# Another order of the first tile, and the last tile in three pieces from two queues

## The chip, the cores and the metric

The kernel runs on one core of one Trainium2 chip. The metric is the device time of one execution in microseconds (us). Lower is better.

## The reference

`x` has the shape (64, 64, 1024): batch, head, length. Each head has a state-space filter of 64 complex states, and each batch element a valid length. The filtered rows go through a feed-forward part with 64 experts of rank 16, of which each row takes the best 16. The result is added to `x`.

```python
u_m = u * mask[:, None, :]                       # mask: position < length
dt = exp(log_dt); A = -exp(log_A_real) + 1j * A_imag
K = 2 * real(einsum('hn,hnl->hl', C * (exp(A * dt) - 1) / A, exp(A * dt * arange(L))))
y = causal_convolution(u_m, K) + u_m * D         # by FFT in the reference
y = y * mask
scores = y @ Wr.T                                # 64 scores for each row of 1024
gates = softmax(top_k(scores, 16)) scattered to 64 columns, the others zero
h = einsum('nd,krd->nkr', y, A)                  # 1024 -> 64 x 16
out = x + 2 * einsum('nkr,kdr->nd', h * gates, B)
```

## The kernel before

**Tiles.** A tile holds two heads (`HT = 2`) of all 64 batch elements, which makes 128 rows; there are 32 tiles (`TILES`). A row of 1024 is cut into 8 chunks of 128 (`NC`).

**The convolution.** For tile t, ACT writes arguments (`theta`), DVE takes them to one turn (`arguments`), ACT makes sines and decays, DVE multiplies them to `powers` (`make_powers`) and to `out_raw` (`out_factors`). TensorE turns the powers (`turn_in`), sums `out_raw` to the filter's first 128 values, the kernel row (`whole_row`, later `kernel_row`), and feeds the states (`whole_feed`, `feed`). ACT copies the row to `k_sb` (`copy_k`), DVE adds the skip weight D to one element per head (`add_skip`), and SP starts two DMAs (`load_near`) that read `k_sb` shifted by one element for each of 128 partitions, and so write the Toeplitz matrix `t_lo`. Then TensorE convolves the chunk with itself (`near`, for tile 0 `whole_near_0`) and adds what the states carry over from earlier chunks (`from_states`, `whole_from_states_0`). DVE steps the states from chunk to chunk (`first_states`, `states`, each step some 1.3 us long in two heads). `mask_y` (for tile 0 `mask_first`) writes the masked rows `y_m`.

**The feed-forward part.** TensorE multiplies `y_m` by the A weights and the router in three column ranges (`H_PARTS`, n = 0, 1, 2). DVE finds the gates (`gate`, `gates_of`) and multiplies each range by them (`gate_part`, into `hg`). TensorE turns `hg` (`turn_hg`), ACT and DVE split it into `g_hi` and `g_lo` (`low_gated`), and TensorE multiplies by the B weights into `out_ps`, in halves of 512 columns (`down_high`, `down_low`). `add_rows` scales, adds x, and SP stores the rows.

**Precision.** From tile 2 on, every product is three products of rounded parts (high by high, high by low, low by high). Tiles 0 and 1 (`EXACT = 2`) use whole float32 operands for A and the convolution, and split ones for B. So all weights have to be split in the first two tiles: ACT rounds a piece to its high part (`split_weights`), DVE subtracts it from the original for the low part (`low_weights`). There are 17 pieces: the router, eight of A, eight of B. Four pieces of B (`EARLY`) have their low parts made by TensorE instead (`whole_b`: the identity times the piece, plus minus the identity times its high part), and ACT copies them out of PSUM.

**Order.** Everything is written out by hand. SP issues the loads in the order of `EARLY`, five of the first pieces, `load_near(0)`, the rest of A, `MIDST` (the other four of B), the x rows. Each engine's queue is in order, and semaphores link them. TensorE begins with `whole_b(0)`, then alternates pieces of B with the first tile's row and feed, does `whole_near_0` and `whole_from_states_0(0)`, and goes on with `first_step` (tile 0's products, the convolution of tile 1, the preparation of tile 2), `step(1, whole=True)`, then a loop of `step(t)`. The last tile runs the same `step` without convolution.

## Time and profile before

| | |
|---|---|
| median of three runs | 953.88 us (953.48 to 954.99) |
| profiled execution, whole time | 952.23 us |
| its span, first to last instruction | 950.4 us |
| TensorE busy | 924.9 us, 97% of the span |
| VectorE (DVE) busy | 701.0 us, 74% |
| ScalarE (ACT) busy | 393.0 us, 41% |
| mean granted TensorE clock | 0.996 of full |

The span is what the profiler sees of the program; 1.8 us of the whole time lie outside it. The busy time of an engine is the union of its instructions, and the page names for idle time what ended it. "PE" is TensorE's matmuls, "PEld" its weight loads, which overlap them. "ACTq" and "SPq" are the engines' instruction queues, where they issue DMAs. A float32 matmul is two instructions in the trace.

### The profile page before, as it was taken

The page shows a single profiled execution, that of the slowest core. Times are in us where ns is not written, and L with a number is a line of the kernel's source. Part 1 is how long each engine was busy: PE and PEld are TensorE (multiplying, and loading weights), DVE is VectorE, ACT ScalarE, POOL GpSimd, SP SyncE. Part 2 cuts the span into 40 slices and gives each one's busy share as a digit, 9 for nine tenths or more (in the row PEclk, how much of TensorE's full clock was granted, in tenths as well). Part 3 has the DMA queues.
Part 4 walks back from the last instruction along what each step waited for, and adds up shares of the span by engine and source line. Part 5 has one row for each costly group of instructions (what it writes and reads, how often), then busy time and mean ns, then how long its engine had stood idle before and what let it go on. Part 6 is the DMA issues. An engine that isn't in the chain of part 4 may idle for free.

```text
span 950.4 us, 15672 instructions
## 1 busy us (share of the span) xinstructions
PE 924.9 (97%) x4772; PEld 819.2 (86%) x4772; DVE 701.0 (74%) x2443; ACT 393.0 (41%) x685; POOL 2.0 (0%) x12
## 2 busy tenths in 40 slices
PE   4899999999999999999999999999999999999998
PEld 2567888899998899998899998889999889999887
DVE  7678977787777788777778777778877778877642
ACT  4655344334344434344434434443534443443210
POOL 0000000000000000000000000000000000000000
PEclk9999999999999999999999999999999999999999
DMA  6713232222332222332222333222233222233211
GB/s 220 227 28 73 53 81 50 56 64 56 72 72 50 48 68 50 72 72 51 49 66 52 68 72 70 51 48 69 50 72 72 50 48 67 50 72 72 34 40 45
DMA packets 27983, 63.60 MB, mean 67 GB/s; under 512 B 5184, under 2 KB 13504, under 8 KB 27968
## 3 DMA queue, kind: packets, MB, share of 16 engines
q1 hardware_dynamic: 27696, 63.29, 30.0%
q8 instruction: 7, 0.11, 0.0%
q10 hardware_dynamic: 272, 0.13, 0.0%
q14 instruction: 8, 0.07, 0.0%
HBM read 42.43 MB, written 16.78 MB: 62 GB/s over the span
## 4 chain that ended last, share of the span: by engine, by line
PE 93%; DVE 4%; DMA 1%; ACT 1%; issue 0%; ACTq 0%; SPq 0%; DVEq 0%
PE out_ps L926 23%; PE h_ps L926 18%; PE out_ps L930 12%; PE h_ps L930 9%; PE turn_ps L926 7%; PE turn_ps L930 4%; PE turn_ps L948 3%; PE h_ps L935 2%; PE conv_ps L881 1%; PE conv_ps L880 1%; PE conv_ps L879 1%; PE conv_ps L863 1%; PE conv_ps L890 1%; PE conv_ps L891 1%; PE conv_ps L864 1%; PE conv_ps L862 1%
## 5 line engine op out<-in xcount | busy, mean ns | idle before, releaser
L926 PE MATMUL out_ps<-b_hi,g_hi 128*128 128x512 f32 x512 | 203.3, 397 | 0.2 <-ACT g_hi L401 0.2
L926 PE MATMUL out_ps<-b_lo,g_hi 128*128 128x512 f32 x512 | 201.1, 393 | 0.0
L743 DVE SCALAR_TENSOR_TENSOR x_in<-out_ps,gate_scale,x_in 128x512 f32<-128x512 f32 x64 | 48.0, 750 | 160.5 <-PE out_ps L930 160.4
L926 PE MATMUL h_ps<-a_hi,y_hi 128*128 128x384 f32 x480 | 163.3, 340 | 0.0
L926 PE MATMUL h_ps<-a_lo,y_hi 128*128 128x384 f32 x480 | 161.6, 337 | 0.0
L930 PE MATMUL out_ps<-b_hi,g_lo 128*128 128x512 f32 x512 | 127.3, 391 | 0.0
L930 PEld LDWEIGHTS out_ps<-b_hi,g_lo 128*128 128x128 f32 x512 | 96.1, 188 | 21.2
L926 PEld LDWEIGHTS out_ps<-b_hi,g_hi 128*128 128x128 f32 x512 | 96.3, 188 | 19.4 <-ACT g_hi L401 0.5
L926 PEld LDWEIGHTS out_ps<-b_lo,g_hi 128*128 128x128 f32 x512 | 96.3, 188 | 19.2
L542 DVE SCALAR_TENSOR_TENSOR z<-swapped,step_other,part 128x64 f32<-128x64 f32 x384 | 92.4, 282 | 11.4
L535 DVE SCALAR_TENSOR_TENSOR part<-z,step_own,conv_ps 128x64 f32<-128x64 f32 x384 | 90.4, 277 | 8.6
L930 PE MATMUL h_ps<-a_hi,y_lo 128*128 128x384 f32 x480 | 94.4, 338 | 0.0
L926 PEld LDWEIGHTS h_ps<-a_lo,y_hi 128*128 128x128 f32 x480 | 90.1, 188 | 0.0
L926 PEld LDWEIGHTS h_ps<-a_hi,y_hi 128*128 128x128 f32 x480 | 90.0, 187 | 0.0
L930 PEld LDWEIGHTS h_ps<-a_hi,y_lo 128*128 128x128 f32 x480 | 85.3, 188 | 0.0
L401 ACT ACTIVATE g_hi<-turn_ps 128x512 fp32r<-128x512 f32 x64 | 38.3, 601 | 113.2 <-PE turn_ps L948 113.2
L335 ACT ACTIVATE k_sb<-h_ps 1x256 f32<-1x256 f32 x31 | 11.7, 376 | 148.7 <-PE h_ps L850 144.4
L926 PE MATMUL turn_ps<-a_hi,y_hi 128*128 128x320 f32 x240 | 71.0, 309 | 1.7 <-DVE a_lo L571 1.7
L926 PE MATMUL turn_ps<-a_lo,y_hi 128*128 128x320 f32 x240 | 70.8, 309 | 0.0
L343 ACT ACTIVATE z_hi<-z 128x896 fp32r<-128x896 f32 x30 | 28.6, 954 | 87.0 <-DVE z L542 87.0
L391 ACT ACTIVATE exp_all<-score_sb,neg_max 128x64 f32<-128x64 f32 x32 | 11.2, 348 | 116.8 <-DVE neg_max L700 116.8
L537 DVE STREAM_SHUFFLE swapped<-z 128x128 f32<-128x128 f32 x192 | 57.0, 297 | 0.0
(198 smaller groups left out, 1504.9 us busy)
## 6 DMA issues: line engine op xcount, KB each, us to landing
xt_in<-in_xt SPq DMA_DIRECT2D x32, 512.0 KB, 3.3
x_in<-in_x SPq DMA_DIRECT2D x64, 256.0 KB, 3.7
out<-x_in SPq DMA_DIRECT2D x62, 256.0 KB, 4.3
b_in<-in_b_t SPq DMA_DIRECT2D x8, 512.0 KB, 8.5
a_in<-in_a_t SPq DMA_DIRECT2D x8, 512.0 KB, 7.6
t_lo<-k_sb SPq DMA_DIRECT2D x64, 64.0 KB, 5.5
out<-x_in SPq DMA_DIRECT2D x4, 128.0 KB, 2.3
a_in<-in_wr_t SPq DMA_DIRECT2D x1, 256.0 KB, 9.0
```

The costliest lines, as they stand in the source:

```text
L335: act.activation(k_sb[:, :, PAD:PAD + P], source[0:1, :, :], ACT.Copy).then_inc(s_kcopy, 1)
L343: act.activation(z_hi[:, :, :, :], z[:, :, :, :], ACT.Copy).then_inc(s_zhi, 1)
L391: act.activation(exp_all[:, :], score_sb[:, :], ACT.Exp, bias=neg_max[:, :]).then_inc(s_exp, 1)
L401: act.activation(g_hi[:, 4 * bank:4 * bank + 4, :].rearrange("p c n -> p (c n)"), turn_ps[:, bank, :], ACT.Copy).then_inc(s_ghi, 1)
L535: dve.scalar_tensor_tensor(out=part[:, i, :], in0=z[:, c - 1, i, :], scalar=step_own[:, bass.ds(n + i, 1)], in1=conv_ps[i][:, c * B:(c + 1 ...
L537: dve.stream_shuffle(swapped[:, :, :], z[:, c - 1, :, :], SWAP).then_inc(s_swap, 1)
L542: dve.scalar_tensor_tensor(out=z[:, c, i, :], in0=swapped[:, i, :], scalar=step_other[:, bass.ds(n + i, 1)], in1=part[:, i, :], op0=ALU.mu ...
L743: dve.scalar_tensor_tensor(out=x_in[:, columns], in0=out_ps[:, half, :], scalar=gate_scale[:, :], in1=x_in[:, columns], op0=ALU.mult, op1= ...
L926: pe.matmul(o, hi[:, c, :], moving[:, c, columns], start=first and c == order[0] and moving is w_hi, stop=False)
L930: last = pe.matmul(o, lo[:, c, :], w_hi[:, c, columns], start=False, stop=c == order[-1])
L935: return pe.matmul(o, y_m[:, c, :], a_in[:, c, c0:c0 + width], start=c == 0, stop=c == NC - 1)
L948: last = pe.transpose(turn_ps[:, c // 4, (c % 4) * P:(c % 4 + 1) * P], hg[:, c * P:(c + 1) * P], ident[:, :])
```

## The change

Five things change together.

1. The first arguments are made by ACT (`theta(0)`), no longer by two DVE instructions; `phases` goes. DVE does the weights alpha and beta before anything of the far steps, which move behind `out_factors(0)`. TensorE does `turn_in(0)`, `whole_row(0)`, `whole_feed(0)` before any piece of B. ACT copies the row before it makes `far_sin`. The load of the lengths and the first split of a weight move behind `theta(0)` in ACT's queue.
2. `k_sb` is on all 128 partitions. `load_near` reads head 0 from partition 0 and head 1 from partition 64.
3. The first tile's convolution is done in halves: `whole_near_0(0)`, `whole_from_states_0(0)`, `whole_near_0(1)`.
4. `EARLY` is one piece of B instead of four. The other seven are `MIDST`, and DVE makes their low parts. The loads have a new order: that piece, seven of router and A, `load_near(0)`, three of B, the last two of A, four of B. ACT splits nine pieces (router and A) in tile 0's step: two before `g_hi`, seven behind `theta(3)`. DVE's and TensorE's orders in `first_step` change too: `turn_hg` in two parts between products.
5. The last tile has a `last_step` of its own: the first `turn_hg` lies inside the third range of the A product, and the output is made in three pieces (`ENDS`: 512, 256 and 256 columns, the last in `h_ps`). Each piece is stored by two DMAs, head 0 from SP, head 1 from ACT.

```diff
-        k_sb = sb("k_sb", [1, HT, KROW])
+        k_sb = sb("k_sb", [P, HT, KROW])
...
+        ENDS = [(out_ps[:, 0, :], slice(0, HALF)), (out_ps[:, 1, 0:HALF // 2], slice(HALF, HALF + HALF // 2)),
+                (h_ps[:, 0, 0:HALF // 2], slice(HALF + HALF // 2, D))]
...
-        EARLY = [FIRST_B + c for c in (4, 5, 6, 7)]
-        MIDST = [FIRST_B + c for c in (3, 2, 1, 0)]
+        EARLY = [FIRST_B + c for c in (4,)]
+        MIDST = [FIRST_B + c for c in (5, 6, 7, 3, 2, 1, 0)]
         LATE = list(range(FIRST_B))
-        HIGH = EARLY + LATE[:3] + MIDST + LATE[3:]
+        HIGH = EARLY + MIDST + LATE
...
-                    row = k_sb[:, i, :]
+                    row = k_sb[i * B:i * B + 1, i, :]
...
-            for i in range(5):
+            for i in range(7):
                 load_weights(i)
             load_near(0, first=True)
-            for i in range(5, FIRST_B):
-                load_weights(i)
-            for i in MIDST:
+            for i in MIDST[:3] + LATE[7:] + MIDST[3:]:
                 load_weights(i)
...
-                    for half in range(2):
-                        sp.wait_ge(s_o, 2 * t + half + 1)
-                        columns = slice(half * HALF, (half + 1) * HALF)
-                        for i in range(HT):
-                            sp.dma_start(rows(out, t, i)[:, columns], x_in[i * B:(i + 1) * B, columns]).then_inc(s_out, 16)
+                    for n, (_, columns) in enumerate(ENDS):
+                        sp.wait_ge(s_o, 2 * t + n + 1)
+                        sp.dma_start(rows(out, t, 0)[:, columns], x_in[0:B, columns]).then_inc(s_out, 16)
...
-                act.activation(k_sb[:, :, PAD:PAD + P], source[0:1, :, :], ACT.Copy).then_inc(s_kcopy, 1)
+                act.activation(k_sb[:, :, PAD:PAD + P], source, ACT.Copy).then_inc(s_kcopy, 1)
...
-            act.dma_start(len_i[:, :], length.partition_broadcast(P)).then_inc(s_len, 16)
-            split_weights(EARLY[0])
             act.wait_ge(s_rates, 1)
...
+            theta(0)
+            act.dma_start(len_i[:, :], length.partition_broadcast(P)).then_inc(s_len, 16)
+            split_weights(EARLY[0])
             sines(0)
+            whole_in(0, in_ps)
+            copy_k(0)
             act.wait_ge(s_far, 1)
             act.activation(far_sin[:, :, :], far_turn[:, :, :], ACT.Sin, scale=TWO_PI).then_inc(s_farwave, 1)
             theta(1)
-            whole_in(0, in_ps)
-            split_weights(EARLY[1])
             low_weights(0)
-            split_weights(EARLY[2])
-            copy_k(0)
-            low_weights(1)
-            split_weights(EARLY[3])
-            low_weights(2)
-            low_weights(3)
-            for i in LATE[:3] + MIDST[:2]:
+            for i in MIDST[:3]:
                 split_weights(i)
             sines(1)
+            decays(1)
             theta(2)
-            decays(1)
-            for i in MIDST[2:] + LATE[3:6]:
+            for i in MIDST[3:]:
                 split_weights(i)
...
                     copy_k(1, k_ps_1)
+                    for i in LATE[:2]:
+                        split_weights(i)
...
                 if first:
-                    for i in LATE[6:]:
-                        split_weights(i)
+                    decays(2)
                     sines(2)
                     theta(3)
-                    decays(2)
+                    for i in LATE[2:]:
+                        split_weights(i)
...
+            for n, (_, columns) in enumerate(ENDS):
+                act.wait_ge(s_o, 2 * (TILES - 1) + n + 1)
+                act.dma_start(rows(out, TILES - 1, 1)[:, columns], x_in[B:HT * B, columns]).then_inc(s_out, 16)
...
-            for i in range(HT):
-                dve.scalar_tensor_tensor(out=args[:, i], in0=grid[:, :].unsqueeze(1).to_broadcast([P, 2, W]), scalar=turns[:, i:i + 1],
-                                         in1=phases[:, :, :], op0=ALU.mult, op1=ALU.add).then_inc(s_theta, 2)
...
             first_states(0)
-            states(0, range(1, 2))
-            add_skip(0)
-            states(0, range(2, 5))
+            states(0, range(1, 3))
...
+            states(0, range(3, 4))
             mask_first(0)
-            states(0, range(5, FED))
+            states(0, range(4, FED))
             arguments(1)
-            for i in MIDST[:2]:
+            mask_first(1)
+            for i in MIDST[:3]:
                 low_weights(i)
-            mask_first(1)
             make_powers(1)
             out_factors(1)
-            for i in MIDST[2:]:
+            for i in MIDST[3:5]:
                 low_weights(i)
...
                 sum_gates()
+                arguments(2)
+                low_weights(MIDST[5])
                 first_states(1)
+                states(1, range(1, 2))
                 add_skip(1)
-                states(1, range(1, 3))
+                low_weights(MIDST[6])
                 gate_part(0, 2)
-                states(1, range(3, 5))
                 low_gated(0, 0)
+                states(1, range(2, 4))
                 low_gated(0, 1)
-                states(1, range(5, FED))
-                arguments(2)
+                states(1, range(4, FED))
...
+                        if n == 2 and c == NC - 2:
+                            pe.wait_ge(s_hg, 2)
+                            turn_hg((7, 6, 5, 4)).then_inc(s_turn, 1)
...
-                pe.wait_ge(s_hg, 3)
-                turn_hg((7, 6, 5, 4)).then_inc(s_turn, 1)
-                turn_hg((3, 2, 1, 0)).then_inc(s_turn, 1)
                 pe.wait_ge(s_ghi, 1)
                 pe.wait_ge(s_kcopy, 2)
+                pe.wait_ge(s_wlo, 3)
+                down_high(0, (4, 5, 6, 7), first=True)
+                pe.wait_ge(s_hg, 3)
+                turn_hg((3, 2, 1, 0)).then_inc(s_turn, 1)
+                down_high(1, (4, 5, 6, 7), first=True)
+                pe.wait_ge(s_ghi, 2)
                 pe.wait_ge(s_wlo, len(MIDST))
-                for half in range(2):
-                    down_high(half, (4, 5, 6, 7), first=True)
-                pe.wait_ge(s_ghi, 2)
                 down_high(0, (0, 1, 2, 3))
...
+            def last_step(t):
+                pe.wait_ge(s_yhi, HT * (t - EXACT) + HT)
+                pe.wait_ge(s_glo, 2 * t)
+                pe.wait_ge(s_ylo, HT * (t - EXACT) + HT)
+                for n, (o, c0, width, _) in enumerate(H_PARTS):
+                    columns = slice(c0, c0 + width)
+                    product_high(o, y_hi, a_hi, a_lo, columns, range(NC), first=True)
+                    if n == 2:
+                        pe.wait_ge(s_hg, 3 * t + 2)
+                        turn_hg((7, 6, 5, 4)).then_inc(s_turn, 1)
+                    product_low(o, y_lo, a_hi, columns, range(NC)).then_inc(s_up, 1)
+                pe.wait_ge(s_ghi, 2 * t + 1)
+                pe.wait_ge(s_o, 2 * t)
+                for n, (o, columns) in enumerate(ENDS):
+                    if n == 1:
+                        pe.wait_ge(s_hg, 3 * t + 3)
+                        turn_hg((3, 2, 1, 0)).then_inc(s_turn, 1)
+                    product_high(o, g_hi, b_hi, b_lo, columns, (4, 5, 6, 7), first=True)
+                pe.wait_ge(s_ghi, 2 * t + 2)
+                for n, (o, columns) in enumerate(ENDS):
+                    product_high(o, g_hi, b_hi, b_lo, columns, (0, 1, 2, 3))
+                    if n == 0:
+                        pe.wait_ge(s_glo, 2 * t + 2)
+                    product_low(o, g_lo, b_hi, columns, (4, 5, 6, 7, 0, 1, 2, 3)).then_inc(s_down, 1)
+
             pe.wait_ge(s_ident, 2)
             pe.wait_ge(s_minus, 3)
+            turn_in(0)
+            whole_row(0, k_ps)
+            whole_feed(0)
             whole_b(0)
-            turn_in(0)
-            whole_b(1)
-            whole_feed(0)
-            whole_row(0, k_ps)
-            whole_b(2)
-            whole_b(3)
-            whole_near_0()
+            pe.wait_ge(s_t, 16 * HT)
+            whole_near_0(0)
             whole_from_states_0(0)
+            whole_near_0(1).then_inc(s_near, 1)
             first_step()
...
-            step(TILES - 1, conv=False, prep=False)
+            last_step(TILES - 1)
```

## Rows read from the trace of the kernel before

**Rows 1.** The page: busy time, share of the span, instructions of TensorE.

```profile
PE 924.9 (97%) x4772; PEld 819.2 (86%) x4772; DVE 701.0 (74%) x2443; ACT 393.0 (41%) x685; POOL 2.0 (0%) x12
```

**Rows 2.** Waits of TensorE in the whole span: us in total, times, longest.

```profile
PE turn_ps L835 <- ACT b_hi L289: 10.9, 1, 10.9
PE out_ps L899 <- DMA t_lo<-k_sb: 3.2, 1, 3.2
...
PE turn_ps L926 <- DVE a_lo L571: 1.7, 1, 1.7
```

**Rows 3.** Windows: stretch, length, busy time by engine, PEclk, DMA share, GB/s.

```profile
36.40:73.50 37.10, 35.23 (x134) 24.07 (x135) 28.52 (x96) 24.49 (x38) 0.00 (x0) 1.00 0.36 95
...
162.50:190.70 28.20, 28.20 (x152) 25.64 (x151) 21.32 (x75) 12.01 (x22) 0.00 (x0) 1.00 0.28 60
```

**Rows 4.** Timeline of TensorE, the first 37 us: start, us, instruction, idle before.

```profile
17.03 1.66 PE L835 MATMUL out_ps<-b_in,ident 128*128 128x512 f32 x2 [1.79 <-ACT b_hi L289]
...
20.98 1.67 PE L872 MATMUL conv_ps<-xt_in,in_whole 128*128 128x448 f32 x4
22.48 0.59 PE L854 MATMUL h_ps<-out_raw,real 128*128 128x256 f32 x2
22.91 1.02 PE L835 MATMUL turn_ps<-b_in,ident 128*128 128x512 f32 x2
...
31.20 3.63 PE L899 MATMUL out_ps<-xt_in,t_lo 128*128 128x256 f32 x8 [3.25 <-DMA t_lo<-k_sb]
...
36.44 0.78 PE L935 MATMUL turn_ps<-a_in,y_m 128*128 128x320 f32 x2 [0.96 <-issue]
```

**Rows 5.** Timeline of ACT: one instruction of `theta`, and the row's copy.

```profile
14.12 0.48 ACT L303 ACTIVATE args<-grid,phase_own,turns 128x130 f32<-128x130 f32 x1
...
23.11 0.38 ACT L335 ACTIVATE k_sb<-h_ps 1x256 f32<-1x256 f32 x1 [4.23 <-PE h_ps L854]
```

**Rows 6.** Timeline of DVE up to 42 us.

```profile
10.67 0.89 DVE L618 SCALAR_TENSOR_TENSOR args<-grid,turns,phases 128x260 f32<-128x260 f32 x2
...
18.48 0.61 DVE L492 SCALAR_TENSOR_TENSOR out_raw<-powers,alpha,out_raw 128x130 f32<-128x130 f32 x2
...
24.14 0.14 DVE L506 TENSOR_TENSOR k_sb<-k_sb,skip 1x2 f32<-1x2 f32 x1
...
39.83 2.35 DVE L571 TENSOR_TENSOR b_lo<-b_in,b_hi 128x1024 fp32r<-128x1024 f32 x2
```

**Rows 7.** DMA between 24 and 32 us, in 40 slices of 0.2 us.

```profile
GB/s 0 0 0 0 0 0 0 18 28 33 26 26 26 23 23 23 26 23 31 28 23 26 28 23 26 23 28 23 23 28 82 149 274 448 369 430 410 471 348 430
```

**Rows 8.** Windows: the stretch in which `whole_near_0` runs.

```profile
31.20:34.50 3.30, 3.30 (x8) 2.67 (x9) 0.00 (x0) 0.28 (x1) 0.00 (x0) 0.50 1.03 420
```

**Rows 9.** Timelines in `first_step` and at the start of `step(1)`.

```profile
46.09 2.94 ACT L289 ACTIVATE a_hi<-a_in 128x1024 fp32r<-128x1024 f32 x3
...
55.44 1.09 PE L948 MATMUL turn_ps<-ident,hg 128*128 128x128 f32 x8 [1.11 <-DVE hg L723]
...
70.86 1.22 DVE L515 TENSOR_TENSOR xt_lo<-xt_in,xt_hi 128x1024 fp32r<-128x1024 f32 x1
...
73.50 4.47 PE L935 MATMUL turn_ps<-a_in,y_m 128*128 128x320 f32 x16
```

**Rows 10.** Two matmuls of 256 columns behind each other.

```profile
99.19 0.28 PE L849 MATMUL h_ps<-o_hi,real 128*128 128x256 f32 x1
99.30 0.28 PE L850 MATMUL h_ps<-o_lo,real 128*128 128x256 f32 x1
```

**Rows 11.** The last tile: timelines of TensorE, DVE and SP.

```profile
934.61 0.66 PE L948 MATMUL turn_ps<-ident,hg 128*128 128x128 f32 x4 [0.21 <-DVE hg L723]
...
946.40 0.75 DVE L743 SCALAR_TENSOR_TENSOR x_in<-out_ps,gate_scale,x_in 128x512 f32<-128x512 f32 x1 [2.80 <-PE out_ps L930]
947.18 1.11 SPq L252 DMA_DIRECT2D out<-x_in  x2
```

**Rows 12.** Groups by line and form from 890 us on: a DVE instruction on 256 columns.

```profile
L723 DVE TENSOR_TENSOR hg<-turn_ps,gates 128x256 f32<-128x256 f32 x2 | 0.8, 425 | 0.1
```

More of the change, by code:

```diff
@@ L295, in low_weights @@
                 for half in range(2):
-                    act.activation(lo[:, half * HALF:(half + 1) * HALF], REST_PS[n][:, half, :], ACT.Copy).then_inc(s_blo, 1)
+                    act.activation(lo[:, half * HALF:(half + 1) * HALF], turn_ps[:, half, :], ACT.Copy).then_inc(s_blo, 1)
             def theta(t):
-                act.wait_ge(s_sine, t)
+                if not (isinstance(t, int) and t == 0):
+                    act.wait_ge(s_sine, t)
                 for i in range(HT):
@@ L668, in _ @@
             out_factors(0)
+            link(dve.tensor_scalar(far[:, 1, :], turns[:, :], float(P), None, ALU.mult))
+            dve.tensor_scalar(whole[:, 1, :], far[:, 1, :], ROUND, ROUND, ALU.add, ALU.subtract)
+            link(dve.tensor_scalar(far[:, 0, :], far[:, 1, :], 0.25, None, ALU.add))
+            link(dve.tensor_scalar(whole[:, 0, :], far[:, 0, :], ROUND, ROUND, ALU.add, ALU.subtract))
+            dve.tensor_tensor(out=far_turn[:, :, :], in0=far[:, :, :], in1=whole[:, :, :], op=ALU.subtract).then_inc(s_far, 1)
+            add_skip(0)
             dve.wait_ge(s_farwave, 2)
@@ L772, in first_step, with step @@
                 add_rows(0, 1)
-            def step(t, conv=True, prep=True, table=True, weights=()):
+            def step(t, conv=True, prep=True, table=True, weights=(), last=False):
                 if conv:
@@ L811, in step @@
                 scale_of(t)
+                if last:
+                    for n in range(len(ENDS)):
+                        add_rows(t, n, ENDS)
+                    return
                 add_rows(t, 0)
@@ L822, in _ @@
             step(TILES - 2, prep=False, table=False)
-            step(TILES - 1, conv=False, prep=False, table=False)
+            step(TILES - 1, conv=False, prep=False, table=False, last=True)
         @block.tensor
@@ L834, in whole_b @@
                     columns = slice(half * HALF, (half + 1) * HALF)
-                    pe.matmul(REST_PS[n][:, half, :], ident[:, :], arrived[:, columns], start=True, stop=False)
-                    last = pe.matmul(REST_PS[n][:, half, :], minus[:, :], hi[:, columns], start=False, stop=True)
+                    pe.matmul(turn_ps[:, half, :], ident[:, :], arrived[:, columns], start=True, stop=False)
+                    last = pe.matmul(turn_ps[:, half, :], minus[:, :], hi[:, columns], start=False, stop=True)
                 last.then_inc(s_rest_ps, 1)
@@ L891, in from_states, with whole_near_0 @@
                     pe.matmul(later, o_lo[:, i, 1:P + 1], z_hi[:, :, i, :], start=False, stop=True).then_inc(s_conv, 1)
-            def whole_near_0():
-                pe.wait_ge(s_t, 16 * HT)
-                pe.wait_ge(s_blo, 2 * len(EARLY))
-                for n in range(2):
-                    columns = slice(n * HALF // 2, (n + 1) * HALF // 2)
-                    for i in range(HT):
-                        last = pe.matmul(conv_0[n][:, i, :, :], t_lo[:, i, :].bitcast(F32), xt_in[:, i, columns],
-                                         start=i == 0, stop=False, skip_group_check=True)
-                last.then_inc(s_near, 1)
+            def whole_near_0(n):
+                columns = slice(n * HALF // 2, (n + 1) * HALF // 2)
+                for i in range(HT):
+                    last = pe.matmul(conv_0[n][:, i, :, :], t_lo[:, i, :].bitcast(F32), xt_in[:, i, columns],
+                                     start=i == 0, stop=False, skip_group_check=True)
+                return last
             def whole_from_states_0(n):
@@ L958, in first_step @@
                 pe.wait_ge(s_w[0], 16)
+                pe.wait_ge(s_blo, 2 * len(EARLY))
                 pe.wait_ge(s_ym0, HT)
```

53 lines of the change are left out of this document (19 added, 34 removed).

## The prediction

> **What bounds the kernel now.** I read the page first: TensorE is busy 97% of the span [rows 1]. Then I asked where its missing 25.5 us lie, by its waits over the whole span [rows 2] and by windows [rows 3]. In the loop there is nothing to win: of a stretch of 28.20 us TensorE is busy 28.20 [rows 3]. No row of waits belongs to the loop either. So the time is TensorE's work, plus what it stands still in the first 106 us, plus the tail behind its last matmul. The waits at the start are 10.9 us for the first piece of B, 3.2 us for `t_lo`, 1.7 us for `a_lo` [rows 2] and some smaller ones. Third I followed the timelines of the first 37 us. TensorE works early, but on pieces of B; the chain that counts is another: kernel row at 22.48 [rows 4], its copy at 23.11 [rows 5], the skip weight at 24.14 [rows 6], the load of `t_lo`, the convolution at 31.20, the products of tile 0 at 36.44 [rows 4]. From there to the loop TensorE is nearly full, so what is gained ahead of 36.44 counts, less what later waits take back.
>
> **Part 1, the row first.** The turns are ready at 10.55. The two instructions on `args`, 0.89 us [rows 6], leave DVE; five small ones on the far steps (0.7 together) move behind. ACT makes the arguments instead: behind the sine table, which it can load earlier since the first split of B (1.0 us) is no longer ahead, it does two sines, then four of `theta` at 0.4 us each [rows 5], so they are there at about 12.7. DVE has by then done the weights up to the fraction (13.3 or so), so it doesn't wait; it ends `out_raw` at about 17.8 instead of 19.1 [rows 6]. Ahead of TensorE's row there is now no piece of B and no feed. The row takes 0.59 us at the full clock [rows 4]; TensorE has only just begun, so I take 1.0. It ends at 18.9, where it ended at 23.07. Copy 0.38, skip 0.14 and the gaps between them [rows 5, 6] put the issue of the load at 19.6 instead of 24.3: 4.7 us earlier. The next work of TensorE, feed (1.67) and `whole_b(0)` (2.2: two halves, each little more than the 1.02 of its first two instructions [rows 4]), ends at 24 to 26 us, by the clock. The lengths' load moved behind `theta(0)` is 32 KB that took 5.9 us to land; DVE needs it at 25, so it costs nothing; without that cover it would be DVE that waits.
>
> **Part 2, two partitions.** The two transfers move 128 KB in 5.3 us, from 25.7 to about 31, at 18 to 33 GB/s, while the weights behind them go at 348 to 471 [rows 7]. The source is one partition, and both transfers go one after the other through the same rings. From two partitions they could overlap, but only as far as engines run ahead into the second: the rate rises from 28 to 448 over some 0.8 us at the end [rows 7], which is how far apart they finish. I take 0.5 us; the bounds are nothing and 2.1 (half of 5.3, less the 0.6 by which the second is issued later). So `t_lo` is there at 31.2 - 4.7 - 0.5 = 26.0. The Trainium skill (SBUF — State Buffer, Door 1: The DMA port swizzle) says that partitions 64 apart lie on different ports of 27.2 GB/s each. The row's rate agrees with one port; no row here shows two. By that rule, with both ports in use at once, the 128 KB would take 2.4 us, an estimate from its figure; what the rows make of such an overlap is rival (c). `k_sb` on 128 partitions costs ACT nothing that a row shows: the same copy with more partitions is what every other ACT row is.
>
> **Part 3, halves.** `whole_near_0` took 3.63 us at half the clock [rows 4, 8]; a matmul of 256 columns at the full clock takes 0.11 a pass [rows 10], and a whole one two passes, so 1.8 for all eight. TensorE now does half (0.9), the states (0.6), then the other half (0.9) while DVE masks the first. Before, it stood 0.96 us for that mask [rows 4]. With `t_lo` at 26.0 the first half and states end at 27.5, the second half and the mask (0.7) at 28.4: the products start at 28.4 instead of 36.4, 8.0 us earlier. DVE would be ready for the mask at about 26.9 (feed ended 22, three steps of the states, the mask's making), so more than 0.6 us cannot come from a faster `t_lo`. The clock: before, TensorE stood 3.25 us and ran the convolution at 0.50 [rows 4, 8], and it stood 1.79 before 17.03 [rows 4] and ran those pieces slowly too. Now it stands up to 2 us. I take the full clock and keep 1.5 us for the other case (0.9 for half the convolution, 0.6 for its states).
>
> **Part 4, the weights.** DVE gets three more pieces of B, at 2.35 us for two [rows 6] 3.5 us, and one more step of the states (1.3) falls behind the first mask. From that mask to the end of `xt_lo` at 72.1 [rows 9] DVE was busy some 28 us (28.52 in [rows 3], less its last 1.4, plus the mask); now 32.7. It had 8.5 us of idleness in that stretch, so the queue takes it, but DVE is now what times it. Piece by piece: masks and states to 33.8; three pieces of B to 37.3; powers and `out_raw` to 38.9; two pieces to 41.2. TensorE's range 0 is done at 38.8, so the gates start 2.4 us late (before, 1.3). That is hidden, since TensorE has ranges 1 and 2, feed and row until 46.6. Then the fixed order bites: arguments, a piece of B, first states, a step, the skip, another piece, and only then the third `gate_part`, at 49.9, while TensorE wants to turn at 48.5: it waits 1.4. The wait of 1.11 at 55.44 [rows 9] goes in exchange, and so does most of the turning behind it. The convolution of tile 1 waits 0.7 for the last steps of the states. ACT has seven splits of A (0.98 each by 2.94 for three [rows 9], 6.8) behind `theta(3)`; queued behind them are `o_hi`, `in_hi`, `xt_hi`, which come at 63.7 at the latest, so `xt_lo` ends at 64.9, and TensorE's feed, ready at 64.3, waits 0.6. `step(1)` starts at 66.1 instead of 73.50 [rows 9]: of the 8.0 us, 0.6 are given back, 7.4 stay. Loads: behind `t_lo` go 4.5 MB of weights, the x rows and `xt` of tile 1, at 0.4 MB per us [rows 7]; a half MB takes 1.3 us, so the last of A lands at 32.7 (needed at 37), the last of B at 37.8, `xt` at 39.7 (needed at 41.5). In `step(1)` the nine `a_lo` are the same, behind the same `turn_hg`, so that wait of 1.7 stays.
>
> **Part 5, the tail.** The first `turn_hg` moves into the product (0.44 in place of a wait of about as much), the second lies between pieces and waits for nothing, so the idle 0.21 and the ramp behind it [rows 11] go: 0.4 us. The 48 matmuls of 256 columns cost as much as 24 of 512, at 0.11 each [rows 10]; the bound on the other side is a pass of 320 columns, 0.14 (4.47 for 16 instructions of two passes [rows 9]), which would add 1.4 us. The last scaling is half as wide: 0.75 [rows 11] becomes 0.43 [rows 12]. One issue is left on each queue: 1.11 for two [rows 11] becomes 0.56. The landing of 2.1 us stays. Sum: 0.4 + 0.3 + 0.55 = 1.3 us less. The bounds are 1.8 less, were the landing half a microsecond shorter for half the bytes, and 0.1 more, with the narrow passes at 0.14.
>
> **The sum.** 7.4 + 1.3 = 8.7 us. The profiled execution of 952.2 us becomes 943.5. The three runs have a median 1.7 us above it, 953.88; so the forecast is 945.2 us. A measurement of this kernel tells 0.2%, 1.9 us, from no change.
>
> **The rivals.** (a) The forecast, 0.52: 945.2, by itself 943.8 to 946.8. (b) The clock is down when `t_lo` comes, 0.18: 1.5 us later masks, and DVE's queue passes it on whole: 946.7. For it: 1.79 us of idleness was enough once [rows 4]. Against: the new gap is shorter if `whole_b` runs slowly. (c) Both rows are read side by side, 0.12: `t_lo` at 31.2 - 4.7 - 2.1 = 24.4; DVE caps it at 0.6 us: 944.6, or 943.1 if my DVE times are late. (d) The queues behind take more: ACT's seven splits, or a load that misses its time by 1.3 us per half MB, hold feed or gates of tile 0 by 2 to 4 us more than I have, 0.10: 948.5. (e) The narrow matmuls run at 0.14, or the small stores land later, 0.05: 946.7 to 947.5. (f) Slower: the loop. If the wider `k_sb` made the row late in each tile, the 29 tiles would repeat it. It decides from 0.4 us a tile (11.6 us): 956. It needs the copy, the skip or the load to eat the slack of `t_lo`, and TensorE has no idle time in a tile that would show it near [rows 3]: 0.03.
>
> **Range and chances.** (a), (b), (c) and (e) lie within 943.0 to 947.5; the upper end goes to 948.8 to take in most of (d). Faster 0.94, same 0.03, slower 0.03.
>
> **What would show it.** Right: TensorE's order row, feed, one piece; the issue of `t_lo` at 19 to 20 us, the first half at 25 to 27, the products at 28 to 29, `step(1)` at 65 to 67.5; `hg` or `xt_lo` as the new short waits; 3.2 us from the last matmul to the end of the span, instead of 4.0. Wrong: a PEclk of 0.50 around 26 to 30 us, a wait for a load at the ranges of A, matmuls of 256 columns further apart than 0.12, a tile of the loop longer than 28.2.

## The result, and the profile after

The changed kernel takes 943.02 us (median of four runs, 942.97 to 943.06), against 953.68 us for the kernel before in the same job (953.11 to 954.99). The ratio is 0.9886, interval 0.9869 to 0.9903. In a second job it took 943.06 us (942.96 to 943.16), against 951.43 for the kernel before (median of 23 runs, 950.52 to 954.99), ratio 0.9906. The forecast was 945.2 with a range of 943.0 to 948.8. The kernel is faster, as forecast, and its time is 2.2 us below the forecast: at the very edge of the range, and below the 943.8 to 946.8 that the forecast had by itself. The gain is 10.7 us where 8.7 were forecast.

The profiled execution took 942.97 us with a span of 941.2, against 952.23 and 950.4: 9.26 us less. The waits of TensorE over its whole span come first, in the columns of [rows 2]:

```profile
PE h_ps L838 <- DVE powers L479: 16.2, 1, 16.2
PE turn_ps L918 <- DVE a_lo L571: 1.7, 1, 1.7
PE out_ps L891 <- DMA t_lo<-k_sb: 1.3, 1, 1.3
PE conv_ps L867 <- issue: 1.2, 1, 1.2
PE conv_ps L908 <- DVE part L535: 0.7, 1, 0.7
PE turn_ps L940 <- DVE hg L714: 0.6, 1, 0.6
PE conv_ps L857 <- issue: 0.6, 1, 0.6
```

TensorE waits longer at the very start (16.2 us, where 10.9 stood in [rows 2]), since it no longer does pieces of B there. The wait for `t_lo` has fallen from 3.2 to 1.3, and the wait for `a_lo` stayed. Behind it stand short new waits: `hg`, `part`, and two that the profile puts down to nothing ("issue"). Of these the 1.2 us are for the load of `xt` (`e8_xt_early` below takes them away), and the 0.6 us end at 64.10, just behind DVE's `xt_lo` (from 62.77, 1.23 us long). The timeline of TensorE, for [rows 4]:

```profile
17.47 1.22 PE L849 MATMUL h_ps<-out_raw,real 128*128 128x256 f32 x2 [0.57 <-DVE out_raw L492]
18.49 2.75 PE L867 MATMUL conv_ps<-xt_in,in_whole 128*128 128x448 f32 x4
21.08 1.02 PE L830 MATMUL turn_ps<-b_in,ident 128*128 128x512 f32 x2
...
24.72 1.13 PE L891 MATMUL out_ps<-xt_in,t_lo 128*128 128x256 f32 x4 [1.30 <-DMA t_lo<-k_sb]
25.69 0.81 PE L901 MATMUL out_ps<-z,out_raw 128*128 128x192 f32 x4
26.34 1.03 PE L891 MATMUL out_ps<-xt_in,t_lo 128*128 128x256 f32 x4
27.55 0.78 PE L927 MATMUL turn_ps<-a_in,y_m 128*128 128x320 f32 x2 [0.19 <-DVE y_m L559]
...
42.17 1.74 PE L867 MATMUL conv_ps<-xt_in,in_whole 128*128 128x448 f32 x4 [1.25 <-issue]
...
65.39 4.47 PE L927 MATMUL turn_ps<-a_in,y_m 128*128 128x320 f32 x16
```

The order is row, feed, one piece of B, half the convolution, states, other half. The products start at 27.55 where they started at 36.44, and `step(1)` at 65.39 where it started at 73.50 [rows 9]. Of 8.89 us gained ahead of the products, 0.78 are given back up to `step(1)`. The loop is the same, and so is the clock, by these windows of the kernel after (columns of [rows 3]):

```profile
36.00:65.39 29.39, 26.87 (x106) 18.35 (x105) 25.08 (x81) 20.80 (x33) 0.00 (x0) 1.00 0.29 66
154.40:182.60 28.20, 28.20 (x152) 25.64 (x151) 21.35 (x75) 12.02 (x22) 0.00 (x0) 1.00 0.26 60
```

DVE is busy 25.08 of the 29.39 us ahead of `step(1)`, 85%, where it was 28.52 of 37.10 [rows 3], 77%. The end, for [rows 10] and [rows 11]; the first two rows are matmuls of the last piece:

```profile
936.67 0.28 PE L918 MATMUL h_ps<-b_hi,g_hi 128*128 128x256 f32 x1
...
936.79 0.28 PE L918 MATMUL h_ps<-b_lo,g_hi 128*128 128x256 f32 x1
...
938.07 0.48 DVE L734 SCALAR_TENSOR_TENSOR x_in<-h_ps,gate_scale,x_in 128x256 f32<-128x256 f32 x1 [1.43 <-PE h_ps L922]
```

DVE starts the last scaling at 938.07, 3.1 us before the span ends at 941.2; before, it started at 946.40 [rows 11], 4.0 before the end at 950.4.

### The profile page after: what moved, and what is told of

It is laid out like the page before. It is cut to its first block, busy times and chain, and to the rows that moved or that the text cites. A ratio compares the mean times of both kernels' runs of the same rounds, so it can differ in the third digit from the quotient of the medians.

```text
span 941.2 us, 15678 instructions
## 1 busy us (share of the span) xinstructions
PE 914.9 (97%) x4778; PEld 815.3 (87%) x4778; DVE 704.8 (75%) x2442; ACT 389.1 (41%) x681; POOL 2.0 (0%) x12
## 4 chain that ended last, share of the span: by engine, by line
PE 92%; DVE 6%; DMA 1%; issue 0%; ACT 0%; ACTq 0%; SPq 0%; DVEq 0%
PE out_ps L918 23%; PE h_ps L918 18%; PE out_ps L922 12%; PE h_ps L922 9%; PE turn_ps L918 8%; PE turn_ps L922 4%; PE turn_ps L940 3%; PE conv_ps L876 1%; PE conv_ps L875 1%; PE conv_ps L874 1%; PE conv_ps L857 1%; PE conv_ps L858 1%; PE conv_ps L885 1%; PE conv_ps L859 1%; PE conv_ps L886 1%; PE conv_ps L884 1%
## 5 line engine op out<-in xcount | busy, mean ns | idle before, releaser
L922 PE MATMUL out_ps<-b_hi,g_lo 128*128 128x512 f32 (+1 forms) x512 | 126.4, 389 | 0.0
L335 ACT ACTIVATE k_sb<-h_ps 128x256 f32<-128x256 f32 x31 | 12.0, 387 | 144.9 <-PE h_ps L845 143.5
```

What stands on the lines that cost most here:

```text
L335: act.activation(k_sb[:, :, PAD:PAD + P], source, ACT.Copy).then_inc(s_kcopy, 1)
L922: last = pe.matmul(o, lo[:, c, :], w_hi[:, c, columns], start=False, stop=c == order[-1])
```

## The experiments

Each stands beside runs of the kernel before in the same job; the jobs ran on three chips. The kernel after itself ran in two jobs only, 943.02 us in the first and 943.06 in the second (`e1_tail_alone` to `e4_after_again`). Where a run of a later job is compared with it, the difference leans on how close these two are, and on the profile. "Products" is the start of tile 0's products on TensorE, "step(1)" that of `step(1)`, both in the profile. Dummy matmuls, where a kernel has them, write to PSUM that nothing reads; the rest of the computation is as it was.

### The parts by themselves: tail, partition, halves, pieces of B

Part 1, the row first, has no run of its own. Its worth is read from the timelines alone.

**`e1_tail_alone`**: the kernel before with part 5 of the change only (`ENDS`, `last_step`, the stores from ACT).

```diff
-                add_rows(t, 0)
...
+                if last:
+                    for n in range(len(ENDS)):
+                        add_rows(t, n, ENDS)
+                    return
```

> The kernel before with part 5 alone (the last tile in three pieces, two queues). Theory: the tail is additive, since its trace in the changed kernel ends 3.2 us behind the last matmul where it ended 4.0 before: 1.1 us less than the kernel before in the profiled span, nothing else moves. Rival (the narrow matmuls cost more than they bring, and the gain of the tail belongs to the start): no difference, within 0.3 us. If the changed kernel's further gain over my sum lies in the tail, this shows over 2 us.

Measured: 949.88 us (949.36 to 953.75, 12 runs) against 951.43, ratio 0.999 (0.9979 to 1.0001). The medians differ by 1.5 us, but both scatter by over 4. The profile is sharper: from the start of `step(1)`, 72.06, to the end of the span, 947.8, there are 875.7 us, where there were 876.9 before (950.4 less 73.50). The tail is worth 1.2 us, 1.1 in the kernel after (941.2 less 65.39 is 875.8). The same profile holds a surprise: nothing at the start had changed, and yet `step(1)` came 1.4 us earlier than in [rows 9]. Here are windows over the second piece of B, which stands ahead of feed and row in TensorE's queue, first of the kernel before, then of this one:

```profile
17.50:20.80 3.30, 3.30 (x6) 0.50 0.44 170
```

```profile
17.50:20.80 3.30, 3.30 (x10) 1.00 0.43 166
```

One execution has the clock at 0.50 (1.2 GHz) there and does six instructions, the other has 1.00 (2.4 GHz) and does ten. The kernel row follows: 22.48 in [rows 4], 21.15 here.

**`e2_one_partition`**: the kernel after, both heads' rows read from partition 0.

```diff
-                    row = k_sb[i * B:i * B + 1, i, :]
+                    row = k_sb[0:1, i, :]
```

> The changed kernel, but both rows of k_sb are read from partition 0. Theory: two source partitions let the two transfers overlap, 3.8 us instead of 5.3; undone, t_lo lands 1.5 us later at 26.2, the first mask waits for it, and the time is 1.2 us longer (1.5 less the 0.3 that DVE was not ready anyway), more if TensorE's clock falls in the longer wait (up to 1.5 more). Rival (the shorter load comes from an idle DMA system, not from the partitions): the load still takes 3.8 us and the time does not change.

Measured: 944.43 to 944.49 in four runs, 945.72 and 945.75 in two, against 943.06 for the kernel after. Timeline of TensorE in one of the longer kind, and the window of its second half of the convolution:

```profile
26.23 1.13 PE L891 MATMUL out_ps<-xt_in,t_lo 128*128 128x256 f32 x4 [2.93 <-DMA t_lo<-k_sb]
27.20 1.42 PE L901 MATMUL out_ps<-z,out_raw 128*128 128x192 f32 x4
28.41 1.91 PE L891 MATMUL out_ps<-xt_in,t_lo 128*128 128x256 f32 x4
```

```profile
28.10:29.90 1.80, 1.80 (x6) 0.50 1.04 426
```

`t_lo` comes 1.5 us later than in the kernel after (26.23 against 24.72), and behind a wait of 2.9 us the clock fell to 0.50 at about 27 us; `step(1)` is at 68.16. So the second partition is worth 1.4 us by itself, and it takes away a further risk: rival (b), at 1.3 us, happened in two runs of six here and in none of the nine runs of the kernel after.

**`e7_no_halves`**: the kernel after, whole convolution first, then the states.

```diff
-            whole_from_states_0(0)
             whole_near_0(1).then_inc(s_near, 1)
+            whole_from_states_0(0)
```

> The changed kernel with both halves of whole_near_0 ahead of the states' part. Theory: TensorE stands for the mask again and the mask comes 0.9 us later; DVE's queue passes 0.9 us on to the end: 943.9. Rival (DVE's later slack takes it): under 0.3 us.

Measured: 943.82 us (943.77 to 943.93), 0.8 more than the kernel after. Its timeline:

```profile
24.70 1.99 PE L891 MATMUL out_ps<-xt_in,t_lo 128*128 128x256 f32 x8 [1.09 <-DMA t_lo<-k_sb]
26.53 0.81 PE L901 MATMUL out_ps<-z,out_raw 128*128 128x192 f32 x4
28.39 0.78 PE L927 MATMUL turn_ps<-a_in,y_m 128*128 128x320 f32 x2 [1.05 <-DVE y_m L559]
```

The wait for the mask is 1.05 us, where it is 0.19 in halves, and the products come 0.84 later. The halves are worth just that, and it reaches the end whole: `step(1)` is at 66.21, 0.82 later.

**`e12_four_by_tensor`**: the main thing of part 4 undone in the kernel after: four pieces of B by TensorE, the loads in their old order. The place of ACT's splits of A and the divided `turn_hg` stay as in the change. The cut shows the pieces alone.

```diff
-        EARLY = [FIRST_B + c for c in (4,)]
+        EARLY = [FIRST_B + c for c in (4, 5, 6, 7)]
...
             whole_b(0)
+            whole_b(1)
+            whole_b(2)
+            whole_b(3)
```

> The changed kernel with part 4 undone: four pieces of B by TensorE ahead of the convolution, the loads in their old order, no piece of B for DVE in tile 0's step. Theory: the convolution starts at 30 instead of 24.7 us, but DVE has 3.5 us less, so TensorE times the stretch: step(1) at 69 to 70 instead of 65.4, 4 us longer (947). Rival (part 4 brings nothing, since DVE gets what TensorE loses): within 1.5 us of 943.0.

Measured: 947.04 us (946.66 to 947.73), 4.0 more than the kernel after. The first half of the convolution stands at 31.11 behind the pieces, 6.4 later than in the kernel after, the products at 33.84, `step(1)` at 70.13. Of 6.3 us of TensorE's work in front of the products 4.7 reach `step(1)`, in a profiled execution of 947.73, the longest of the six; the other 1.6 come back before `step(1)`.

**`e11_two_by_tensor`**: the same with two pieces (`EARLY` of 4 and 5).

> The changed kernel with two pieces of B by TensorE instead of one. Theory (DVE times the stretch, and TensorE stands 1.3 us before t_lo anyway): DVE has 1.15 us less, TensorE's second piece ends 0.7 us after t_lo; together 0.3 to 0.6 us shorter. Rival (TensorE's time ahead of the convolution is the scarcer): 0.5 us or more longer.

Measured: 943.34 us (942.87 to 943.89, 5 runs), no difference that this spread can tell from 943.06. The second piece lies in the wait for `t_lo`, which is gone; the half starts at 25.40 instead of 24.72, the products at 28.13 instead of 27.55, and `step(1)` at 65.29 instead of 65.39. DVE has one piece less, and what the products lose comes back in its queue. One piece or two is even here.

### What holds tile 0's stage

**`e8_xt_early`**: in the kernel after, `xt` of tile 1 loaded ahead of the last two pieces of B and of the x rows.

```diff
-            for i in MIDST[:3] + LATE[7:] + MIDST[3:]:
+            for i in MIDST[:3] + LATE[7:] + MIDST[3:5]:
                 load_weights(i)
-            fetch_rows(0)
             sp.wait_ge(s_near, 1)
             load_x(1)
+            for i in MIDST[5:]:
+                load_weights(i)
+            fetch_rows(0)
```

> The changed kernel, with the load of xt of tile 1 ahead of the last two pieces of B and the x rows. In the profile that load took 13.3 us and TensorE stood 1.25 us for it at 40.9. Theory (DVE's third gate_part at 49.0 is what TensorE would wait for instead): the wait at 40.9 goes, one of 1.0 to 1.3 appears ahead of the second turn_hg, and the time stays within 0.2 us. Rival (the load binds): 0.9 to 1.25 us shorter.

Measured: 943.0 us (942.94 to 943.36), no change. Its waits of TensorE:

```profile
PE turn_ps L942 <- DVE hg L716: 1.6, 2, 1.0
PE conv_ps L910 <- DVE part L537: 0.7, 1, 0.7
PE conv_ps L859 <- issue: 0.6, 1, 0.6
```

The wait of 1.2 us for `xt` is gone, and 1.0 us more are waited for `hg`; `step(1)` starts at 65.39 as before. The load was late, but the stage is timed by DVE. **`e4_after_again`**, the kernel after unchanged in the second job, says the same by chance:

> The changed kernel unchanged, for the size of the difference on this chip and the spread. Theory A: 943.0 within 0.2 us in every run, and the runs of the kernel before between 952 and 955.5, with the lower granted clock in the longer ones. Rival B: the runs of before differ without a difference of clock.

There the load came earlier (its wait was 0.36 us), `hg` was waited for 0.73, and `step(1)` was at 65.42. Its five runs lie within 0.2 us, as theory A had it; those of the kernel before go down to 950.52, below the 952 of the theory, and the longest have the lowest clock (0.994 from 953.05 us on).

**`e3_before_filled`**: the kernel before with three dummy matmuls of 512 columns in its wait for `t_lo`.

```diff
             whole_b(3)
+            for _ in range(3):
+                pe.matmul(h_ps[:, 0, :], ident[:, :], xt_in[:, 0, :], start=True, stop=True)
             whole_near_0()
```

> The kernel before, with three matmuls of 512 whole columns (2.8 us, result unused) in the time in which TensorE waits for t_lo, so that its clock does not fall. Theory A (the clock at half in whole_near_0 cost the kernel before 1.8 us there, and where its windows fall differs from run to run, which is the spread of 1.9 us in its runs): whole_near_0 takes 1.8 instead of 3.6 us, the time is 1.5 to 2 us shorter in the profile, up to 2.5 in the median, and the runs lie within 0.3 us of each other. Rival B (the spread is of DMA or of the start, not of the clock): whole_near_0 is shorter but the runs scatter as before by over 1 us.

Measured: 951.43 us (950.32 to 953.84, 12 runs), the same as the kernel before. The wait was filled and the clock stayed up, and it bought nothing; nor did the runs draw together, as rival B had it. They lie 3.5 us apart, and the three shortest (950.32 to 950.68) and the two longest (953.54 and 953.84) all have a mean granted clock of 1.00. Timeline, and waits of TensorE, in the profiled execution (950.86 us):

```profile
30.13 1.99 PE L899 MATMUL out_ps<-xt_in,t_lo 128*128 128x256 f32 x8 [0.66 <-DMA t_lo<-k_sb]
```

```profile
PE turn_ps L948 <- DVE hg L723: 1.9, 3, 1.1
...
PE conv_ps L872 <- ACT in_whole L327: 1.0, 1, 1.0
```

The convolution takes 1.99 us instead of 3.63 [rows 4], the products start at 33.74, but `step(1)` at 72.13, the same as with the slow convolution in `e1_tail_alone` (products 34.97, `step(1)` 72.06). A new wait of 1.0 for ACT's `in_whole` takes it. ACT in turn had stood for a piece of B, here until 36.50, and in the kernel before:

```profile
37.55 1.06 ACT L289 ACTIVATE b_hi<-b_in 128x1024 fp32r<-128x1024 f32 x1 [6.07 <-DMA b_in<-in_b_t]
```

That piece is queued on SP behind `load_near(0)`, which waits for the row. So in the kernel before, too, an earlier product is worth nothing by itself: ACT's queue, and the load it stands for, have to be earlier as well. In the change the pieces of B leave TensorE's and ACT's queues at the same place.

### Why the kernel before scatters

Its 23 runs in the second job go from 950.52 to 954.99, the kernel after's five within 0.2 us. `e3_before_filled` above and the next two kernels ask whether TensorE's clock in the first 35 us is the cause; then the same is tried on the kernel after.

**`e5_before_warmed`**: the kernel before with 18 small dummy matmuls at its very start.

> The kernel before, with 18 small matmuls of the identity by itself (result unused) from 3.3 us on, ahead of its first piece of B, so that the clock has risen when the work begins. Theory C (the spread of the kernel before, 950.5 to 955.0, comes from where in its first 20 us the clock rises: the filled wait for t_lo did not remove it, 950.3 to 953.8): the pieces of B run at full clock from the first on, the row ends at 20.5 to 21.5 us, all runs lie within 0.5 us of each other between 949.5 and 951. Rival D (the spread comes from the loads or from DVE and ACT at the start): it stays over 1.5 us wide.

Measured: 953.58 us (952.96 to 955.14, 12 runs) against 952.42, 1.1 longer (ratio 1.0014, interval 1.0001 to 1.0027): the opposite of a gain, and still 2.2 us wide. In the waits between 13.5 and 17.3 us the clock fell again (PEclk 0.83 there, 0.50 from 17.3 to 21.7), the row came at 23.77 and `step(1)` at 74.84. Three executions now stand in a line (`e1_tail_alone`, the kernel before, this one): row 21.15, 22.48, 23.77 and `step(1)` 72.06, 73.50, 74.84. The loads link the two: `t_lo` is issued at 22.98, 24.31 and 25.61, and the piece of B queued behind it, for which ACT stands, is there at 36.20, 37.55 and 38.84, each time 13.2 us later.

**`e9_before_kept_busy`**: dummies also in the two waits ahead of the row and, not in the cut, the three of `e3_before_filled` in that for `t_lo`. "(dummy)" stands for a matmul of the identity by itself.

```diff
             pe.wait_ge(s_minus, 3)
+            for _ in range(18): (dummy)
             whole_b(0)
+            for _ in range(5): (dummy)
             turn_in(0)
+            for _ in range(7): (dummy)
             whole_b(1)
```

> The kernel before with unused small matmuls wherever TensorE waits in the first 31 us: 18 at the start, 5 and 7 around turn_in(0), three wide ones before whole_near_0. The warm-up at the start alone made it longer (953.6), since the clock fell again in the waits at 13.5 to 17.3 and the row came at 23.8 instead of 22.5. Theory C (where the clock stands between 17 and 24 us sets the row's time, and the row's time sets the rest: row at 21.15, 22.48, 23.77 goes with step(1) at 72.06, 73.50, 74.84): the row is at 21.1 in every run, and all runs lie within 0.5 us of 950.3. Rival D: the spread stays over 1.5 us.

Measured: 951.79 us (951.40 to 952.12, 11 runs; a twelfth of 3309.8 is left out), while the kernel before went from 950.31 to 955.19 in the same job. Timeline:

```profile
19.32 1.66 PE L872 MATMUL conv_ps<-xt_in,in_whole 128*128 128x448 f32 x4
20.82 0.59 PE L854 MATMUL h_ps<-out_raw,real 128*128 128x256 f32 x2
...
33.14 0.78 PE L935 MATMUL turn_ps<-a_in,y_m 128*128 128x320 f32 x2 [0.97 <-issue]
```

With the clock up throughout (1.00 in each window to 34.5 us), the scatter is 0.7 us instead of 4.9, and instead of the 3.5 of `e3_before_filled`, which lacks only the dummies ahead of the row. Above 952.12 lie ten of the 17 runs of the kernel before in this job, two of the 12 of `e3_before_filled`, and none here: the long runs go with the waits in which TensorE stood idle, and with its slow pace behind them. That all of this is the granted clock isn't shown: in `e3_before_filled` runs 3.5 us apart have the same mean clock, and of the kernel before in the job of `e5_before_warmed` one run of 951.13 and one of 953.97 both have 0.998.

The level is not as expected: the row is the earliest of all, but `step(1)` is at 72.81, since ACT waits for a piece of B until 37.2 us and TensorE then for `in_whole`, 1.2. That piece comes 14.6 us behind the issue of `t_lo` at 22.64, not 13.2. A later load that binds in this way may also be what evens out the short end of the scatter; the runs don't tell these two apart. The fastest runs of the kernel before are 1.1 to 1.5 us below this kernel; why the load is late here isn't shown.

**`e6_after_warmed`** has 20 dummies ahead of `turn_in(0)` in the kernel after, and **`e10_after_kept_busy`** 22 there, 3 behind it, and 9 behind `whole_b(0)`.

> The changed kernel, with 20 such matmuls from 8.5 us to at most 16 us, ahead of turn_in(0). The profile has row and feed of tile 0 at half the clock (1.0 and 2.75 us instead of 0.5 and 1.5). Theory: DVE times this stretch; the states of tile 0 come 1.5 us earlier and t_lo 0.5 us, so the first mask comes about 0.5 us earlier, and 0.4 to 0.6 us go over to the end (942.5). Rival (DVE has slack there, t_lo or the loads bind): no change within 0.15.

> The changed kernel with 22 unused small matmuls from 8.5 us, 3 before the row, 9 before the wait for t_lo. The warmed one had two kinds of runs, 942.4 and 943.9, and in the profile a wait of 2.4 us for t_lo. Theory (the clock falls in that wait in some runs): all runs at 942.4 within 0.2 us. Rival (another cause of two kinds): both kinds stay.

Measured: `e6_after_warmed` 942.39 and 942.42 in two runs, 943.81 to 943.95 in three. The feed takes 1.67 us instead of 2.75 and the products start at 27.00, which is the gain of 0.6; but an earlier end of TensorE's work makes the wait for `t_lo` 2.4 us, and in three runs the mean clock reads 0.998. `e10_after_kept_busy`: 943.26 us (942.42 to 945.41, 6 runs), two of them at 0.998 and 945.1 or more. Its profile has the products at 27.19 and `step(1)` at 65.44. The products are 0.36 us earlier than in the kernel after and `step(1)` is no earlier: the wait for `xt`, ready at 42.30, has grown to 1.75 us. Filling the waits made the kernel after less steady, 3.0 us wide where it was 0.2; both kinds of runs stayed, as the rival had it, and what lets the clock fall in its two longer runs stays open.

### Two queues, and the three together

**`e14_two_queues`**: in the kernel after, head 1's first transfer of `t_lo` is issued by ACT behind `far_sin`, head 0's by SP as before. The access patterns are shortened to "...".

```diff
-                for i in range(HT):
+                for i in range(1 if first else HT):
...
+            act.wait_ge(s_kdone, 1)
+            act.dma_start(t_lo[:, 1, :]..., k_sb[B:B + 1, 1, :]...).then_inc(s_t, 16)
             theta(1)
```

> The changed kernel with the second row's load of t_lo in tile 0 issued by ACT instead of SP, so that the two transfers needn't go one after the other through the same rings. The two took 5.3 us from one partition and 3.8 from two. Theory (the source partition is the limit, 128 KB at 24.7 GB/s from one, and what is left of the 3.8 is that the rings work through the first before the second): both together in 2.7 to 3.3 us, t_lo 0.3 to 0.8 us earlier; DVE is ready for the mask 0.3 us ahead, so 0.3 us at most reach the end. Rival (3.8 us is a limit of small packets, not of order): the same 3.8 us.

Measured: 943.63 us (943.59 to 943.71), 0.6 longer than the kernel after. Both are issued at 19.40. The median time from issue to landing, in the kernel after, then here:

```profile
t_lo<-k_sb SPq DMA_DIRECT2D x2, 64.0 KB, 4.4
```

```profile
t_lo<-k_sb SPq DMA_DIRECT2D x1, 64.0 KB, 4.0
t_lo<-k_sb ACTq DMA_DIRECT2D x1, 64.0 KB, 6.0
```

SP's half lands at 23.4, ACT's at 25.4, and TensorE starts the convolution at 25.47, where it is 24.72 with both from SP; `step(1)` is at 66.14 for 65.39. Why the second queue is slower here isn't shown; that the weights' traffic shares with it from 22.6 us on is a suspicion.

**`e13_combined`**: two pieces by TensorE, `xt` early, 20 dummies ahead of `turn_in(0)`.

> The changed kernel with three edits of the experiments together: 20 unused small matmuls from 8.5 us, two pieces of B by TensorE, the load of xt of tile 1 ahead of the last two pieces of B. Theory: the small matmuls bring the feed 1.5 us forward (942.4 in the warmed kernel's faster runs), and the second piece fills the 2.4 us in which its clock fell in the other runs. All runs at 942.0 to 942.5. Rival: DVE's and ACT's queues take all of it, 942.9 or more, or two kinds of runs remain.

Measured: 942.31 us (941.82 to 942.68, 4 runs), ratio 0.989 to the kernel before (0.9873 to 0.9906): the lowest median of all, 0.7 below the kernel after in the other jobs. Three of its four runs lie just outside the 942.0 to 942.5 of the theory. The dummies bring `t_lo` forward, the second piece covers the wait (0.20 left, 2.4 in `e6_after_warmed`), and none of the four runs has the clock down:

```profile
24.27 1.13 PE L898 MATMUL out_ps<-xt_in,t_lo 128*128 128x256 f32 x4 [0.20 <-DMA t_lo<-k_sb]
...
64.52 4.47 PE L934 MATMUL turn_ps<-a_in,y_m 128*128 128x320 f32 x16
```

## Why the prediction was right and where it was wrong

Right were the bound (the first 66 us and the tail, nothing in the loop), the sign, and most of the mechanisms; wrong were how far the two transfers overlap, DVE as a cap on the first mask, what holds TensorE in the middle of the stage, and the last step of the sum. The forecast for the profiled execution was 943.5 and it took 942.97. The steps in turn:

**Part 1.** Predicted: `t_lo` issued at 19.6. Measured: 19.34. `out_raw` ends at 17.4 instead of 17.8, the row takes 1.22 us instead of 1.0.

**Part 2.** Predicted: 0.5 us, `t_lo` at 26.0. Measured: 1.5 us in `e2_one_partition`, `t_lo` at 24.7. This is the term that was too small, and `t_lo` is near rival (c), 24.4. That rival (c) also names a time of 943.1 is no hit, since the 1.7 us that failed are in it too. The argument that two transfers of one queue can hardly overlap was the wrong one to stop at. In the slices of 0.2 us between 19 and 27 us of the kernel after,

```profile
GB/s 0 0 0 0 0 0 0 15 31 28 31 23 26 23 26 23 23 38 126 202 266 210 228 248 289 289 190 307 205 246 307 287 328 328 410 307 369 307 410 225
```

the slow stretch is 11 slices, 2.2 us, where [rows 7] have 23 slices, 4.6 us; its rate is the same. At 26 GB/s 2.2 us hold 57 KB, somewhat under half of the 128 KB, so the rest moves while the weights already flow; how it is shared out between the two transfers no row shows. The Trainium skill (SBUF — State Buffer, Door 1: The DMA port swizzle) puts partitions 64 apart on different ports; 2.4 us for both transfers, my estimate from its port rate, would have had `t_lo` some 2.9 us earlier than from one partition. The measured 1.5 lies between that and my 0.5, and no slice of `t_lo` alone shows the rate doubled.

**Part 3.** Predicted: products at 28.4. Measured: 27.55. Of the 1.3 us by which `t_lo` was earlier than forecast, 0.85 passed, since from `t_lo` to the products it took 2.83 us where I had 2.4: 1.62 for the first half and the states, 0.2 until DVE's mask starts at 26.54, 0.76 for the mask and 0.25 behind it. DVE was no cap: I had it ready for the mask at 26.9, and it was idle for 0.27 us before 26.54. `e7_no_halves` puts the halves at 0.8 us, near the 0.96 of [rows 4]. The clock did not fall in the kernel after; `e2_one_partition` shows that rival (b) was real, at 1.3 us where I had 1.5.

**Part 4.** Predicted: 0.6 given back, `step(1)` at 66.1. Measured: 0.78 and 65.39. The waits that I named came, for `hg`, `part` (0.68 for 0.7) and the feed behind `xt_lo` (0.60 for 0.6). The wait for `hg` is 0.64 for 1.4, for a reason that I had wrong: `xt` came at 42.1, not 39.7, and held TensorE before `hg` could. `e8_xt_early` shows that the two are one and the same slack: take the load's away and `hg` grows by it. Together the two waits are 1.89 us where I had 1.4, so the size is near by a path that I had not drawn. It holds because DVE times the stage, as forecast.

**Part 5.** Predicted: 1.3. Measured: 1.1, and 1.2 alone. Passes of 256 columns stand 0.12 us apart, a little over the 0.11 of [rows 10]; over 48 of them that is up to 0.5 us.

**The step that failed** is the last one of the sum: "The three runs have a median 1.7 us above it, 953.88; so the forecast is 945.2". The parts sum to 8.7 us and gave 9.3, half a microsecond short: part 2 alone was 1.0 short, and parts 3 to 5 took some of it back. The 1.7 us weigh three times as much. They are no constant beside the kernel. In the second job the kernel before has a median of 951.43, which is 0.8 below that profiled execution of 952.23: the offset has the other sign there. It is the scatter of the kernel before, whose pace in its first 35 us differs from run to run, as `e1_tail_alone` and `e5_before_warmed` show in rows; `e9_before_kept_busy` takes most of the scatter away by keeping TensorE busy, and how much of it is the granted clock stays open. The kernel after has no piece of B and no wait for one ahead of its row, its runs agree within 0.2 us in each of its two jobs, and its median lies 0.05 above its profiled execution. A sum made against one profiled execution should have stayed at 943.5, or asked where in 950.5 to 955 the profiled execution stood.

## What to carry to other kernels

Before adding the offset between a profiled execution and the median to a forecast, ask what makes the runs of this kernel scatter, and whether the change takes that away: here the offset of 1.7 us was most of an error of 2.2. When a stage is timed by the queue of another engine, price each late load or wait in it against that queue; a wait of 1.2 us for `xt` cost nothing, a mask 0.8 us later cost 0.8. Look, too, at what is queued behind a load that waits: in the kernel before a piece of B followed the row by way of `load_near(0)`. When a small transfer out of one partition is on the path, spread its source over partitions far apart and keep it on one queue, then measure.

## What the runs showed of the hardware

TensorE works slowly in its first microseconds even where the profile grants the full clock. In the kernel after the feed takes 2.75 us (3.19 in `e4_after_again`) and the row 1.22, both at PEclk 1.00; with dummies ahead they take 1.67 and 0.70 (`e6_after_warmed` and `e10_after_kept_busy` alike). The granted clock does not show this; the durations do. So a mean granted clock of 1.00 doesn't say that TensorE was at full pace from the start.

Dummy work in some of the waits can be worse than none: the kernel before took 953.58 us with it at the start alone, 952.42 without in the same job, and, in another, 951.79 with the larger waits of the first 31 us filled and 952.35 without.

A load queued behind others lands late without a sign on its own row: `xt` of tile 1 was issued at 28.77 and ready 13.4 us later (42.17), behind some 5 MB issued since `t_lo`.
